# A decoder layer on one core: softplus by ScalarE's own table, and the scan's pieces moved to other stages

## The chip, the core and the metric

The kernel runs on one core of a Trainium2 chip. The metric is the device time of one execution in microseconds (us), the median of several runs. Engines are named as in the profile: PE is TensorE's matmul (PEld its weight load), DVE is VectorE, ACT is ScalarE, POOL is GpSimd, SP issues DMAs.

## The reference

One decoder layer over four batches `b` of 512 rows by 512 columns, all in float32:

```
x = x + attention(layernorm(x))                      # 16 query heads, 2 key/value heads, causal, rotary
x = x + mamba(ctx, gate=layernorm(x))                # selective scan, 512 channels, 16 states
x = x + ffn(layernorm(x))                            # gate/up/down 1408 wide, 8 experts' adapters, top 2
```

The part that the change touches is the selective scan. With `dt = softplus(dt_low @ dt_proj + bias)` and `u` the convolved input, both 512 channels by 512 positions:

```
dt = jax.nn.softplus(dt + dt_proj_b[None, :, None])
state = state * exp(d[..., None] * A) + (d * u)[..., None] * b[:, None, :]
y = einsum('bdn,bn->bd', state, c)                   # 16 states n
y = (y + D * u) * silu(z)
```

## The kernel before

Every engine has its own program, written out by hand, and semaphores tie them. The time runs through these stages, for batch b (of attention and scan) and t (of the feed-forward part):

1. Batch 0 alone: input projection and convolution of the scan, softplus, and eleven places `down0` to `down10` in which PE projects queries, keys and values and DVE rotates them (`rotate`).
2. `attention(b)`: 32 steps, each a pair of heads by one block of 128 query rows. In a step PE makes scores, DVE takes the negated maximum (L1117), ACT the exponent (L622), PE transposes, ACT copies, and PE weighs the values. Scores for step s wait for the exponents of step s - 2. A group of 8 steps goes through the four query blocks, two steps each, with 1, 2, 3 and 4 blocks of keys.
3. `second_sum(t)`, the router, the adapters' masks.
4. 33 evaluations, three for each of the 11 feed-forward tiles f: k = 0 (the base product), 1 and 2 (with one and two experts' adapters). PE fills PSUM, ACT applies Silu (L674), DVE multiplies (L1253). PE's order is adapter 1 of tile f, base product of tile f + 1 (16 matmuls), adapter 2 of tile f, adapter-down product of tile f - 1, and so on; adapter k of a tile waits for the multiplication of evaluation k - 1.
5. Eleven down products `down0` to `down10`, PE's projections of the next batch between them, DVE's rotations beside them, then `finish(t)`, which adds the result to `xb` (L1266) and releases the score banks for the next attention.

Stages 4 and 5 and the attention of batch t + 1 also carry the scan of batch t + 1, cut into pieces. Each piece is one instruction over all 4 channel tiles, 128 x 2048: `mul` (L1077, du times row B), `run` (L1082, the scan itself), `out` (L1087, times row C), 16 of each. Before them come 12 `poly` pieces, which finish softplus: ACT computes |x|, exp(-|x|) and relu(x) of four tiles (`softplus_parts`, L546, L549, L551), and DVE evaluates log1p(e) by a polynomial of degree 9 (one L1051, nine L1054), adds relu (L1059) and multiplies by u (L1063). `plan(counts)` deals the pieces in this order to slots: the 33 evaluations, 11 down places and 32 attention steps. `PLAN_FIRST` serves batch 0, which has no evaluations before it; `PLAN_NEXT` serves batches 1 to 3. For each state the plan also names the slot in which ACT loads rows B and C (`load_bc`, DMA `bc_sb<-bc_rows`, which waits for `out` of state n - 2), the one in which ACT makes the four decays exp(A dt) (`make_decay`, L580, waits for `run` of state n - 2), and the one in which POOL issues the DMA that adds the state into `y_sb` (L484). `mul` of state n waits for that DMA of state n - 2 and for its own rows.

In a slot DVE's program does the evaluation, the maximum or the rotation first and then its pieces, strictly in order. ACT's program does Silu, then loads rows, then decays. Silu, Exp and Softplus stand in different activation tables; ACT_TABLE_LOAD switches between them.

The attention's normalization of the next batch (`deviation`, a POOL power L474, `scaled` L1024) is done four times, once in each of evaluations 18, 21, 24 and 27 (k = 2 of tiles 5 to 8), with a piece between deviation and scaling.

Of the kernel before, what the change touches and what calls it, by code (L numbers as in the profile page):

```python
# [7 lines left out]
ALU = mybir.AluOpType  # L8
# [6 lines left out]
NT = L // P  # L15
# [7 lines left out]
NS = 16  # L23
# [22 lines left out]
def log1p_coefficients(degree):  # L46
    import numpy as np
    nodes = 0.5 + 0.5 * np.cos(np.pi * (np.arange(64) + 0.5) / 64)
    fit = np.polynomial.Chebyshev.fit(nodes, np.log1p(nodes) / nodes, degree, domain=[0, 1])
    return [float(c) for c in fit.convert(kind=np.polynomial.Polynomial).coef]  # L50


POLY = log1p_coefficients(9)
NPOLY = len(POLY)

# [18 lines left out]
NORM_SLOTS = [EVAL_AT[FT - 2 - NT + i, 2] for i in range(NT)]  # L74
DT_SLOTS = (2, 3)
POLY_AT = 4 
LAST_TILE = FT - 1 
# [15 lines left out]
def plan(counts):  # L93

    pieces = [("poly", k) for k in range(NPOLY + 2)]
    for n in range(NS):
        pieces += [("mul", n), ("run", n), ("out", n)]
    assert sum(counts) == len(pieces), (sum(counts), len(pieces))
    slots, at, k = [{"dve": [], "bc": [], "decay": [], "add": []} for _ in range(SLOTS)], {}, 0
    for s, count in enumerate(counts):  # L100
        for piece in pieces[k:k + count]:
            slots[s]["dve"].append(piece)
            at[piece] = s
        k += count
# [11 lines left out]
PIECES = NPOLY + 2 + 3 * NS  # L116
# [75 lines left out]
def decoder_layer(nc, x, ctx_t, wq, wk, wv, wo, w_in, w_x, w_dt, w_lora, w_r, b_down, a_down, w_tiles, w_adapt, w_down,  # L192
                  vectors, constants, out, bc_rows):
    with ExitStack() as stack:
# [63 lines left out]
        u_sb, exp_v, relu_v, conv_sb = state[:, 0, :, :], state[:, 1, :, :], decay[:, 0, :, :], decay[:, 1, :, :]  # L258
        xin_sb = relu_v
# [64 lines left out]
        softplus_chain = sem("softplus_chain")  # L324
        softplus_in = sem("softplus_in")
        y_init = sem("y_init")
        poly_chain = sem("poly_chain")
# [142 lines left out]
        def _(pool):  # L470
# [27 lines left out]
            for t in range(BATCH - 1):  # L498
                inverse_deviation("ffn", t)
                for e in range(EVALS):  # L500
                    inverse_deviation("att", t + 1, [i for i in range(NT) if NORM_SLOTS[i] == e])
# [8 lines left out]
        def _(act):  # L510
# [31 lines left out]
            def softplus_parts(b, tiles):  # L542
                for j in tiles:
                    bank = filled(act, ("dt", j), b)
                    bias = vec[:, V_DTB + j:V_DTB + j + 1]
# [7 lines left out]
                if JT - 1 in tiles:  # L553
                    act.wait_ge(softplus_chain, (b + 1) * 2 * JT)
                    nc.scalar.activation(scrap_a[:], vec[0:1, 0:1], ACT.Copy).then_inc(softplus_in, 1)
# [136 lines left out]
            softplus_parts(0, range(JT))  # L692
# [7 lines left out]
            for t in range(BATCH - 1):  # L700
# [8 lines left out]
                for e in range(EVALS):  # L709
                    if e > 0:  # L710
                        evaluate(t, e)
                    scan_inputs(t + 1, PLAN_NEXT[e])
                    softplus_parts(t + 1, [j for _, j in dt_uses(e)])
# [294 lines left out]
        def _(dve):  # L1008
# [36 lines left out]
            def scan_piece(b, piece):  # L1045
                kind, n = piece
                if kind == "poly":

                    if n == 0:
                        dve.wait_ge(softplus_in, b + 1)  # L1050
                        ts(du_sb[:], exp_v, POLY[-1], None, ALU.mult).then_inc(poly_chain, 1)  # L1051
                    elif n < NPOLY:
                        dve.wait_ge(poly_chain, b * (NPOLY + 2) + n)
                        stt(du_sb[:].rearrange("p j l -> p (j l)"), du_sb[:].rearrange("p j l -> p (j l)"),  # L1054
                            POLY[NPOLY - 1 - n], exp_v.rearrange("p j l -> p (j l)"), ALU.add, ALU.mult)\
                            .then_inc(poly_chain, 1)
                    elif n == NPOLY:
                        dve.wait_ge(poly_chain, b * (NPOLY + 2) + n)
                        tt(dt_sb[:], du_sb[:], relu_v, ALU.add).then_inc(poly_chain, 1)  # L1059
                    else:  # L1060
                        dve.wait_ge(poly_chain, b * (NPOLY + 2) + n)
                        dve.wait_ge(u_ready, b * JT + JT)
                        tt(du_sb[:], dt_sb[:], u_sb, ALU.mult).then_inc(poly_chain, 1)  # L1063

                        nc.vector.memset(decay[:, :, :, 0:1], 0.0).then_inc(dt_ready, 1)
                    return
                base = b * 3 * NS + 3 * n
                flat = state[:, n % 2, :, :].rearrange("p j l -> p (j l)")
                if kind == "mul":
                    if n == 0:  # L1070
                        dve.wait_ge(poly_chain, (b + 1) * (NPOLY + 2))
# [212 lines left out]
            for t in range(BATCH - 1):  # L1284
# [126 lines left out]
```

## Time and profile before

| | |
|---|---|
| Median of 3 runs | 1597.76 us (1597.14 to 1597.82) |
| The profiled execution's own time | 1596.27 us |
| Its span in the profile | 1594.5 us |
| PE busy | 1382.6 us, 87% |
| DVE busy | 1108.9 us, 70% |
| ACT busy | 689.2 us, 43% |
| POOL busy | 112.0 us, 7% |
| Mean granted TensorE clock | 0.888 of full speed |

Busy shares are means over stages with different limits: in the attention of batch 0 DVE is hardly ever idle, while in the feed-forward part of the last batch, which has no scan beside it, it is idle most of the time. The rows below are therefore read stage by stage.

### The profile page before, as it was taken

How to read it: one execution, taken by the hardware profiler on the slowest of the kernel's cores; microseconds unless marked ns; L12 is line 12 of the kernel's file. 1: busy time of each engine (PE TensorE's matmuls, PEld its weight loads, DVE VectorE, ACT ScalarE, POOL GpSimd, SP SyncE). 2: the span in 40 equal slices, each digit the busy share in tenths (PEclk: the TensorE clock that was granted, in tenths of full speed). 3: DMA queues.
4: the chain of work that ended last, by engine and by line, in shares of the span. 5: the costliest groups of instructions: out<-in, count | busy, mean ns of one | idle time of the engine just before them, and what ended most of it. 6: DMA issues, size and time to landing. Idle time of an engine off the chain costs nothing.

```text
span 1594.5 us, 16051 instructions
## 1 busy us (share of the span) xinstructions
PE 1382.6 (87%) x5768; PEld 675.0 (42%) x5768; DVE 1108.9 (70%) x1247; ACT 689.2 (43%) x1501; POOL 112.0 (7%) x116
## 2 busy tenths in 40 slices
PE   6756667999988799899989699899989698799999
PEld 2334334444443355434444255444434255454443
DVE  4899996557989775737999866637998967621120
ACT  6155653344543484343552376361562277321110
POOL 0000001000200000000210000100210000100000
PEclk8955558999999699999999778999999869789999
DMA  4166662114667631113766722002566751101112
GB/s 191 40 152 157 141 142 50 42 50 112 172 145 172 171 68 27 40 35 81 180 147 159 196 67 54 27 32 80 141 150 152 169 139 28 27 19 61 50 35 84
DMA packets 53277, 158.80 MB, mean 100 GB/s; under 512 B 5072, under 2 KB 10704, under 8 KB 44752
## 3 DMA queue, kind: packets, MB, share of 16 engines
q0 software_dynamic: 9216, 67.11, 20.4%
q1 hardware_dynamic: 25664, 54.23, 10.1%
q10 hardware_dynamic: 18320, 36.45, 8.6%
q8 instruction: 47, 0.77, 0.2%
q14 instruction: 30, 0.25, 0.0%
HBM read 86.20 MB, written 4.46 MB: 57 GB/s over the span
## 4 chain that ended last, share of the span: by engine, by line
issue 30%; PE 29%; DVE 26%; DMA 7%; ACT 5%; POOL 2%; ACTq 0%; DVEq 0%; POOLq 0%
DVE state L1082 10%; DMA y_sb<-state 7%; PE ps_a L890 5%; PE ps_a L970 4%; DVE state L1077 4%; PE ps_w L869 3%; DVE state L1087 3%; PE ps_a L816 3%; PE ps_a L902 2%; PE ps_b L830 2%; ACT r L622 2%; POOL rstd L474 2%; DVE neg_max L1117 2%; PE ps_b L910 2%; PE ps_w L778 2%
## 5 line engine op out<-in xcount | busy, mean ns | idle before, releaser
L890 PE MATMUL ps_a<-xt,w_sb 128*128 128x512 f32 x704 | 316.1, 603 | 0.0
L1082 DVE TENSOR_TENSOR_SCAN state<-decay,state 128x2048 f32<-128x2048 f32 x64 | 282.8, 4419 | 7.5 <-ACT decay L580 3.4
L1253 DVE TENSOR_TENSOR r<-r,ps_a 128x512 f32<-128x512 f32 x132 | 88.6, 683 | 206.4 <-ACT r L674 206.4
L816 PE MATMUL ps_a<-r 32*128 32x512 f32 (+3 forms) x512 | 140.6, 634 | 84.0 <-ACT r L622 57.5
L890 PEld LDWEIGHTS ps_a<-xt,w_sb 128*128 128x128 f32 x704 | 135.6, 194 | 171.1 <-issue 171.1
L674 ACT ACTIVATE r<-ps_a 128x512 f32<-128x512 f32 x132 | 78.4, 597 | 297.8 <-PE ps_a L902 158.7
L580 ACT ACTIVATE decay<-dt_sb,decay_rate 128x511 f32<-128x511 f32 x256 | 163.0, 712 | 63.2 <-DVE state L1087 31.2
L622 ACT ACTIVATE r<-ps_a,neg_max 128x128 f32<-128x128 f32 (+3 forms) x256 | 133.8, 534 | 118.7 <-DVE neg_max L1117 118.3
L902 PE MATMUL ps_a<-r,wb_sb 128*128 128x512 f32 x352 | 166.7, 596 | 11.1 <-DVE r L1253 8.9
L970 PE MATMUL ps_a<-wd_sb,r 128*128 128x512 f32 x352 | 161.8, 611 | 0.8 <-DMA wd_sb<-in_w_down 0.8
L1077 DVE TENSOR_TENSOR state<-du_sb,bc_sb 128x2048 f32<-128x2048 f32 x64 | 146.3, 2287 | 5.2 <-DMA y_sb<-state 5.0
L1087 DVE TENSOR_TENSOR state<-state,bc_sb 128x2048 f32<-128x2048 f32 x64 | 146.0, 2281 | 0.7
L830 PE MATMUL ps_b<-cst,r 128*128 128x128 f32 x640 | 120.4, 331 | 25.6 <-ACT xt L634 17.2
L1117 DVE TENSOR_REDUCE neg_max<-ps_a 128x2 f32<-128x256 f32 (+3 forms) x128 | 104.0, 814 | 19.9 <-PE ps_a L819 19.0
L484 POOL DMA_DIRECT2D y_sb<-state x64 | 56.1, 877 | 738.1 <-DVE state L1087 653.4
L902 PEld LDWEIGHTS ps_a<-r,wb_sb 128*128 128x128 f32 x352 | 64.9, 190 | 101.9 <-issue 95.1
L970 PEld LDWEIGHTS ps_a<-wd_sb,r 128*128 128x128 f32 x352 | 69.1, 198 | 88.7 <-issue 84.0
L830 PEld LDWEIGHTS ps_b<-cst,r 128*128 128x128 f32 x640 | 89.1, 172 | 34.5 <-issue 28.7
L816 PEld LDWEIGHTS ps_a<-r 32*128 32x128 f32 x512 | 50.2, 239 | 120.7 <-ACT r L622 79.7
L474 POOL TENSOR_TENSOR rstd<-var_eps,cst 128x1 f32<-128x1 f32 x48 | 56.0, 1167 | 543.7 <-DVE var_eps L1020 534.3
L910 PE MATMUL ps_b<-r,ad_sb 128*128 128x512 f32 x176 | 85.8, 611 | 1.9 <-DVE r L1253 1.7
L1054 DVE SCALAR_TENSOR_TENSOR du_sb<-du_sb,state 128x2048 f32<-128x2048 f32 x36 | 82.4, 2288 | 0.6
(123 smaller groups left out, 1448.4 us busy)
## 6 DMA issues: line engine op xcount, KB each, us to landing
y_sb<-state POOLq DMA_DIRECT2D x64, 1024.0 KB, 9.7
bc_sb<-bc_rows ACTq DMA_DIRECT2D x64, 512.0 KB, 5.1
w_sb<-in_w_tiles SPq DMA_DIRECT2D x44, 512.0 KB, 4.0
wd_sb<-in_w_down SPq DMA_DIRECT2D x44, 256.0 KB, 3.6
wb_sb<-in_w_adapt SPq DMA_DIRECT2D x44, 128.0 KB, 2.1
xa<-in_x SPq DMA_DIRECT2D x4, 1024.0 KB, 5.2
out_x<-xb SPq DMA_DIRECT2D x16, 256.0 KB, 7.0
xn_att<-in_ctx_t SPq DMA_DIRECT2D x4, 512.0 KB, 6.1
```

The costliest lines, as they stand in the source:

```text
L580: nc.scalar.activation(decay[:, n % 2, j, 1:L], dt_sb[:, j, 1:L], ACT.Exp, scale=decay_rate[:, j, n:n + 1]).then_inc(decay_ready, 1)
L622: nc.scalar.activation(probs[:, (2 * s + k) % 4, 0:(i + 1) * P], score_place(s, k), ACT.Exp, bias=neg_max[:, s % 2, k:k + 1], accum_out=ro ...
L816: nc.tensor.matmul(score_place(s, k), q_t[rows, m, i * P:(i + 1) * P], k_t[rows, 0:width], start=True, stop=False, tile_position=(rows.sta ...
L830: mm = nc.tensor.transpose(ps_b[:, k, kt * P:(kt + 1) * P], probs[:, (2 * s + k) % 4, kt * P:(kt + 1) * P], ident)
L890: mm = nc.tensor.matmul(ps_a[:, 2 * (f % 2) + half, :], w_sb[:, slot, at + k * P:at + (k + 1) * P], xt[:, k, :], start=(k == 0), stop=Fals ...
L902: mm = nc.tensor.matmul(ps_a[:, 2 * (f % 2) + half, :], wb_sb[:, f % 2, at:at + P], low[:, 2 * half + k - 1, :], start=False, stop=(k == 2 ...
L910: mm = nc.tensor.matmul(ps_b[:, k - 1, :], ad_sb[:, f, :], hk[:, (2 * f + k - 1) % 4, :], start=(f == 0), stop=(f == FT - 1), skip_group_c ...
L970: mm = nc.tensor.matmul(ps_a[:, i, :], hb[:, f, i * P:(i + 1) * P], wd_sb[:, f % 2, :], start=(f == 0), stop=False, skip_group_check=True)
L1077: tt(state[:, n % 2, :, :], du_sb[:], row, ALU.mult).then_inc(scan_chain, 1)
L1082: nc.vector.tensor_tensor_scan(flat, decay[:, n % 2, :, :].rearrange("p j l -> p (j l)"), flat, 0.0, ALU.mult, ALU.add).then_inc(scan_chai ...
L1087: tt(state[:, n % 2, :, :], state[:, n % 2, :, :], row, ALU.mult).then_inc(scan_chain, 1)
L1117: nc.vector.tensor_reduce(neg_max[:, s % 2, :], both, AX.X, ALU.max, negate=True)\
```

## The change

Softplus becomes one ACT instruction per tile, straight from PSUM into `dt_sb`, and the 12 poly pieces become one piece `du`. The 49 pieces that are left are dealt anew. The normalization moves to evaluations 1 and 3, two tiles in each.

```diff
-NORM_SLOTS = [EVAL_AT[FT - 2 - NT + i, 2] for i in range(NT)]
+NORM_AT = {EVAL_AT[0, 1]: (0, 1), EVAL_AT[0, 2]: (2, 3)}
...
-    pieces = [("poly", k) for k in range(NPOLY + 2)]
+    pieces = [("du", 0)]
...
-        slots[between(at["poly", NPOLY - 4] if n < 2 else at["out", n - 2], at["mul", n])]["bc"].append(n)
-        slots[between(at["poly", NPOLY + 1] if n < 2 else at["run", n - 2], at["run", n])]["decay"].append(n)
+        slots[at["du", 0] if n < 2 else between(at["out", n - 2], at["mul", n])]["bc"].append(n)
+        slots[between(at["du", 0] if n < 2 else at["run", n - 2], at["run", n])]["decay"].append(n)
...
-IN_EVALS = [(0, 2, 1)[k] if e >= POLY_AT and f <= LAST_TILE else 0 for e, (f, k) in enumerate(EVAL)]
-IN_DOWN = 22 
+IN_EVALS = [0 if f == 0 else ((0, 2, 0) if f == 1 else (0, 2, 1))[k] for f, k in EVAL]
+IN_DOWN = 20
...
-EARLY_FIRST = [5, 5]
-IN_DOWN_FIRST = 13 
-PLAN_FIRST = plan([0] * DOWN + EARLY_FIRST + spread_over(IN_DOWN_FIRST - sum(EARLY_FIRST), FT - 2) +
-                  spread_over(PIECES - IN_DOWN_FIRST, STEPS - LAST_STEPS) + [0] * LAST_STEPS)
+PLAN_FIRST = plan([0] * DOWN + [1] * FT + spread_over(PIECES - FT, STEPS - LAST_STEPS) + [0] * LAST_STEPS)
...
-                    nc.scalar.activation(exp_v[:, j, :], ps_w[:, bank, :], ACT.Abs, bias=bias)\
-                        .then_inc(softplus_chain, 1)
-                    act.wait_ge(softplus_chain, (b * JT + j) * 2 + 1)
-                    nc.scalar.activation(exp_v[:, j, :], exp_v[:, j, :], ACT.Exp, scale=-1.0)\
-                        .then_inc(softplus_chain, 1)
-                    nc.scalar.activation(relu_v[:, j, :], ps_w[:, bank, :], ACT.Relu, bias=bias)\
-                        .then_inc(work_free[bank], 1)
...
+                    nc.scalar.activation(dt_sb[:, j, :], ps_w[:, bank, :], ACT.Softplus,
+                                         bias=vec[:, V_DTB + j:V_DTB + j + 1]).then_inc(work_free[bank], 1)
...
+                if kind == "du":
+
+                    for j in (JT - 2, JT - 1):
+                        bank, count = use(("dt", j), b)
+                        dve.wait_ge(work_free[bank], count + 1)
+                    dve.wait_ge(u_ready, b * JT + JT)
+                    tt(du_sb[:], dt_sb[:], u_sb, ALU.mult).then_inc(du_ready, 1)
...
-                    if e in NORM_SLOTS:
+                    for i in NORM_AT.get(e, ()):
                         dve.wait_ge(loaded["x"], 16 * t + 32)
-                        deviation("att", t + 1, xa, NORM_SLOTS.index(e))
+                        deviation("att", t + 1, xa, i)
+                    for i in NORM_AT.get(e, ()):
+                        scaled("att", t + 1, xa, xn_att, i)
```

What `plan` then gives, with m, r and o for mul, run and out and the state's number:

| | before | after |
|---|---|---|
| batch 0, down0 to down10 | 12 poly (10 of them in down0 and down1), m0 | du, m0, r0, o0, m1, r1, o1, m2, r2, o2, m3, one in each |
| batch 0, attention | r0 to o15, 47 pieces | r3 to o15, 38 pieces |
| batches 1 to 3, evaluations | 12 poly in tiles 1 to 4, then m, r at k = 1 and o at k = 2 of tiles 5 to 10, states 0 to 5 | du, m0 at evaluation 4; r, o at k = 1 and m at k = 2 of tiles 2 to 10: r0 to m9 |
| batches 1 to 3, down | m6 to m13, 22 pieces | r9 to o15, 20 pieces |
| batches 1 to 3, attention | r13, o13, m14, r14, o14, m15, r15, o15 in steps 3, 7, 11, 15, 19, 23, 27, 30 | none |

## Rows read from the trace of the kernel before

**Rows 1.** Busy time by stretch: start:end, length, then PE, PEld, DVE, ACT, POOL, clock, DMA.

```profile
80.10:247.10 167.00, 109.55 (x716) 61.46 (x716) 164.59 (x123) 92.83 (x258) 13.32 (x15) 0.57 0.64 147
375.00:387.30 12.30, 12.30 (x30) 5.39 (x29) 10.80 (x9) 9.25 (x13) 0.00 (x0) 1.00 0.21 61
400.00:412.80 12.80, 12.26 (x29) 5.24 (x28) 12.14 (x13) 6.91 (x9) 3.36 (x2) 1.00 0.70 182
1456.80:1540.90 84.10, 84.10 (x197) 37.24 (x196) 14.39 (x22) 12.54 (x21) 0.00 (x0) 1.00 0.17 54
450.70:537.20 86.50, 69.56 (x166) 30.66 (x164) 79.05 (x46) 25.52 (x39) 6.96 (x8) 0.93 0.69 164
537.20:559.60 22.40, 21.42 (x117) 11.20 (x118) 13.83 (x20) 15.62 (x50) 0.00 (x0) 0.52 0.53 166
559.60:614.20 54.60, 48.00 (x564) 29.34 (x562) 39.69 (x64) 41.87 (x149) 1.74 (x2) 0.96 0.23 50
```

**Rows 2.** Groups of DVE instructions: busy us, mean ns, idle before.

```profile
L1082 DVE TENSOR_TENSOR_SCAN state<-decay,state 128x2048 f32<-128x2048 f32 x64 | 282.8, 4419 | 7.5 <-ACT decay L580 3.4
L1077 DVE TENSOR_TENSOR state<-du_sb,bc_sb 128x2048 f32<-128x2048 f32 x64 | 146.3, 2287 | 5.2 <-DMA y_sb<-state 5.0
...
L1054 DVE SCALAR_TENSOR_TENSOR du_sb<-du_sb,state 128x2048 f32<-128x2048 f32 x36 | 82.4, 2288 | 0.6
```

**Rows 3.** Groups of ACT instructions.

```profile
L674 ACT ACT_TABLE_LOAD x28 | 35.9, 1283 | 0.5
...
L546 ACT ACTIVATE state<-ps_w,vec 128x512 f32<-128x512 f32 x16 | 10.9, 680 | 1.1 <-PE ps_w L752 1.1
...
L549 ACT ACT_TABLE_LOAD x7 | 9.0, 1283 | 0.1
```

**Rows 4.** Timeline of batch 0's softplus, ACT, then DVE: start, duration, [idle before].

```profile
27.16 0.67 ACT L546 ACTIVATE state<-ps_w,vec 128x512 f32<-128x512 f32 x1
...
36.37 1.23 DVE L1051 TENSOR_SCALAR du_sb<-state 128x2048 f32<-128x2048 f32 x1 [9.96 <-ACT scrap_a L555]
```

**Rows 5.** DMA issues of the page: count, KB each, us to landing.

```profile
y_sb<-state POOLq DMA_DIRECT2D x64, 1024.0 KB, 9.7
bc_sb<-bc_rows ACTq DMA_DIRECT2D x64, 512.0 KB, 5.1
```

**Rows 6.** Timeline of evaluation tile 7, DVE and PE.

```profile
407.23 4.42 DVE L1082 TENSOR_TENSOR_SCAN state<-decay,state 128x2048 f32<-128x2048 f32 x1
...
411.57 1.26 DVE L1253 TENSOR_TENSOR r<-r,ps_a 128x512 f32<-128x512 f32 x2
...
412.38 1.96 PE L902 MATMUL ps_a<-r,wb_sb 128*128 128x512 f32 x4 [0.54 <-DVE r L1253]
```

**Rows 7.** Timeline of the down stage of t = 0, DVE and PE.

```profile
469.79 0.69 DVE L1099 TENSOR_TENSOR r<-ps_w,cst 128x512 f32<-128x512 f32 x1 [5.16 <-PE ps_w L785]
...
523.24 2.29 DVE L1077 TENSOR_TENSOR state<-du_sb,bc_sb 128x2048 f32<-128x2048 f32 x1 [0.66 <-DMA y_sb<-state]
...
514.55 1.12 PE L799 MATMUL ps_b<-cst,r 128*128 128x128 f32 x4 [7.03 <-ACT r L608]
...
536.06 0.80 PE L816 MATMUL ps_a<-r 32*128 32x128 f32 x4 [9.10 <-DVE xb L1266]
```

**Rows 8.** Timeline of batch 1's attention, DVE: maxima of steps 14, 16, 18, 20, 22, 24.

```profile
572.19 1.22 DVE L1117 TENSOR_REDUCE neg_max<-ps_a 128x2 f32<-128x1024 f32 x1
...
579.55 0.41 DVE L1117 TENSOR_REDUCE neg_max<-ps_a 128x2 f32<-128x256 f32 x1
...
582.89 0.68 DVE L1117 TENSOR_REDUCE neg_max<-ps_a 128x2 f32<-128x512 f32 x1
...
587.13 0.95 DVE L1117 TENSOR_REDUCE neg_max<-ps_a 128x2 f32<-128x768 f32 x1
...
591.43 1.22 DVE L1117 TENSOR_REDUCE neg_max<-ps_a 128x2 f32<-128x1024 f32 x1
...
596.65 0.42 DVE L1117 TENSOR_REDUCE neg_max<-ps_a 128x2 f32<-128x256 f32 x1
```

More of the change, by code:

```diff
@@ L43 @@
 VD = KV_HEADS * HD
[L46 to L54, printed above, removed]
 EVAL = [(0, 0)]
@@ L72 @@
 SLOTS = ATT + STEPS
-NORM_SLOTS = [EVAL_AT[FT - 2 - NT + i, 2] for i in range(NT)]
+NORM_AT = {EVAL_AT[0, 1]: (0, 1), EVAL_AT[0, 2]: (2, 3)}
 DT_SLOTS = (2, 3)
-POLY_AT = 4
-LAST_TILE = FT - 1
 PV_AT = 5
@@ L113, in spread_over @@
     return [(k + 1) * total // places - k * total // places for k in range(places)]
-PIECES = NPOLY + 2 + 3 * NS
-IN_EVALS = [(0, 2, 1)[k] if e >= POLY_AT and f <= LAST_TILE else 0 for e, (f, k) in enumerate(EVAL)]
-IN_DOWN = 22
+PIECES = 1 + 3 * NS
+IN_EVALS = [0 if f == 0 else ((0, 2, 0) if f == 1 else (0, 2, 1))[k] for f, k in EVAL]
+IN_DOWN = 20
 FREE_DOWN = 1
 LAST_STEPS = 1
-EARLY_FIRST = [5, 5]
-IN_DOWN_FIRST = 13
-PLAN_FIRST = plan([0] * DOWN + EARLY_FIRST + spread_over(IN_DOWN_FIRST - sum(EARLY_FIRST), FT - 2) +
-                  spread_over(PIECES - IN_DOWN_FIRST, STEPS - LAST_STEPS) + [0] * LAST_STEPS)
+PLAN_FIRST = plan([0] * DOWN + [1] * FT + spread_over(PIECES - FT, STEPS - LAST_STEPS) + [0] * LAST_STEPS)
 PLAN_NEXT = plan(IN_EVALS + spread_over(IN_DOWN, FT - FREE_DOWN) + [0] * FREE_DOWN +
@@ L256, in decoder_layer @@
         xdt_sb = sb("xdt_sb", [P, L])
-        u_sb, exp_v, relu_v, conv_sb = state[:, 0, :, :], state[:, 1, :, :], decay[:, 0, :, :], decay[:, 1, :, :]
-        xin_sb = relu_v
+        u_sb, xin_sb, conv_sb = state[:, 0, :, :], decay[:, 0, :, :], decay[:, 1, :, :]
         scrap = sb("scrap", [1, 1])
@@ L323, in decoder_layer @@
         bc_stored = sem("bc_stored")
-        softplus_chain = sem("softplus_chain")
-        softplus_in = sem("softplus_in")
         y_init = sem("y_init")
-        poly_chain = sem("poly_chain")
+        du_ready = sem("du_ready")
         dt_ready = sem("dt_ready")
@@ L500, in _ @@
                 for e in range(EVALS):
-                    inverse_deviation("att", t + 1, [i for i in range(NT) if NORM_SLOTS[i] == e])
+                    inverse_deviation("att", t + 1, NORM_AT.get(e, ()))
                     add_states(t + 1, PLAN_NEXT[e])
@@ L540, in split_first, with softplus @@
                                          scale=vec[:, V_D + j:V_D + j + 1]).then_inc(y_init, 1)
-            def softplus_parts(b, tiles):
+            def softplus(b, tiles):
                 for j in tiles:
                     bank = filled(act, ("dt", j), b)
-                    bias = vec[:, V_DTB + j:V_DTB + j + 1]
-                    nc.scalar.activation(exp_v[:, j, :], ps_w[:, bank, :], ACT.Abs, bias=bias)\
-                        .then_inc(softplus_chain, 1)
-                    act.wait_ge(softplus_chain, (b * JT + j) * 2 + 1)
-                    nc.scalar.activation(exp_v[:, j, :], exp_v[:, j, :], ACT.Exp, scale=-1.0)\
-                        .then_inc(softplus_chain, 1)
-                    nc.scalar.activation(relu_v[:, j, :], ps_w[:, bank, :], ACT.Relu, bias=bias)\
-                        .then_inc(work_free[bank], 1)
-                if JT - 1 in tiles:
-                    act.wait_ge(softplus_chain, (b + 1) * 2 * JT)
-                    nc.scalar.activation(scrap_a[:], vec[0:1, 0:1], ACT.Copy).then_inc(softplus_in, 1)
+                    nc.scalar.activation(dt_sb[:, j, :], ps_w[:, bank, :], ACT.Softplus,
+                                         bias=vec[:, V_DTB + j:V_DTB + j + 1]).then_inc(work_free[bank], 1)
             def scan_inputs(b, slot):
@@ L691, in _ @@
             split_first(0)
-            softplus_parts(0, range(JT))
+            softplus(0, range(JT))
             for f in range(FT):
@@ L712, in _ @@
                     scan_inputs(t + 1, PLAN_NEXT[e])
-                    softplus_parts(t + 1, [j for _, j in dt_uses(e)])
+                    softplus(t + 1, [j for _, j in dt_uses(e)])
                 for f in range(FT):
@@ L1046, in scan_piece @@
                 kind, n = piece
[L1047 to L1065, printed above, removed]
+                if kind == "du":
[4 more added lines that the diff above has]
+                    tt(du_sb[:], dt_sb[:], u_sb, ALU.mult).then_inc(du_ready, 1)
+                    nc.vector.memset(decay[:, :, :, 0:1], 0.0).then_inc(dt_ready, 1)
                     return
@@ L1070, in scan_piece @@
                     if n == 0:
-                        dve.wait_ge(poly_chain, (b + 1) * (NPOLY + 2))
+                        dve.wait_ge(du_ready, b + 1)
                         dve.wait_ge(y_init, b * JT + JT)
@@ L1292, in _ @@
                     evaluate(t, e)
-                    if e in NORM_SLOTS:
+                    for i in NORM_AT.get(e, ()):
                         dve.wait_ge(loaded["x"], 16 * t + 32)
-                        deviation("att", t + 1, xa, NORM_SLOTS.index(e))
+                        deviation("att", t + 1, xa, i)
+                    for i in NORM_AT.get(e, ()):
+                        scaled("att", t + 1, xa, xn_att, i)
                     for piece in PLAN_NEXT[e]["dve"]:
                         scan_piece(t + 1, piece)
-                    if e in NORM_SLOTS:
-                        scaled("att", t + 1, xa, xn_att, NORM_SLOTS.index(e))
                 weigh_down(t)
```

## The prediction

> **What bounds the kernel now.** I read the page first, for its slices: the clock granted to TensorE dips in each attention, and no engine is the bound throughout. So I cut the span into stages [rows 1]. Four things are to be seen there. In the attention of batch 0 DVE is busy for 164.6 of 167.0 us while PE is at 109.6: DVE is the bound. In the evaluations of the last batch, which carry no scan, seven tiles take 84.1 us with PE busy all the time, 12.0 us each: PE is the bound. An evaluation tile with a scan state and a normalization takes 12.8 us with DVE at 12.1; one with a scan state alone takes 12.3 with DVE at 10.8 and PE never idle. The down stage takes 86.5 us with DVE at 79.1 and PE at 69.6: DVE again. The attention of batch 1, with 8 pieces, takes 22.4 us for its first 8 steps, PE at 21.4 and the clock at 0.52, hence nearly all of it at 1.2 GHz, and 54.6 for the steps up to the last maximum, clock 0.96, PE at 48.0, DVE at 39.7, ACT at 41.9: there no engine is full, and the loop from engine to engine is the bound.
>
> **The change, part by part.** A mul, an out and a poly piece cost 2.29 us, a run 4.42 [rows 2], so a state costs 9.0. The 12 poly pieces of a batch are at most 12 x 2.29 = 27.5 us of DVE, du is one product of the same size, 2.3 (I take out, du and mul as equal). So 25 us a batch, about 100 us in all, leave DVE. What that is worth is read stage by stage.
>
> *Batch 0, up to attention.* Softplus: 12 instructions of some 0.68 us [rows 3] become 4. The trace has no Softplus. From below it costs the 0.68 of a 128 x 512 instruction with the same bias, from above the three that it replaces, 2.0. I take 0.68, since shape, source and bias are those of L546. ACT's part runs from 27.2 to 36.4, where DVE gets its first piece after 10.0 us idle [rows 4]; with 8 x 0.65 us less, and PE half waiting on it, it ends near 33. But m0 now waits for rows B and C, which ACT issues only after the four copies that follow softplus, at about 37.5, and which land 5.1 us later [rows 5]: DVE idles from 35.5 to some 42.7. The stage's DVE work is du + 4 mul + 3 run + 3 out = 31.7 us, and rotations and the value copy, 11. From 33: 33 + 31.7 + 11 + 7.2 = 82.9, against 80.1, where attention begins now. So +2.8 us (-3 to +6: the order of bc, decay and copies on ACT can cost or give as much again).
>
> *Batch 0, attention.* Nine pieces fewer, three states: -27.0. DVE idles 2.4 us now; one piece to a step is less even, and with the clock low a step takes 22.4 / 8 = 2.8 us without DVE being the bound, against 3.5 of DVE for a mul with its maximum. I add 2. So -25 (-29 to -16). Together with the line above: **-22 us**.
>
> *Evaluations, three times.* Pieces per tile and slot are the same 6.7 us at k = 1 and 2.3 at k = 2, now in tiles 2 to 10. In the tiles with a normalization the run ends at 411.6, two multiplications follow back to back, and PE has waited 0.54 us for them [rows 6]; DVE's 12.1 + waits fill 12.8. Without the normalization DVE has 10.8, and PE's 12.0 should set the pace. Four tiles give 4 x 0.8 = -3.2. The normalization's new places, evaluations 1 and 3, lie where PE does the dt products and the projection; I count some 4.3 us of DVE and POOL in each, inside idle time of 5 to 6 us. Where that cover is gone, it costs 4.3 once. ACT's Softplus loads stay as many as the Exp loads they replace (7), and Silu's return is the same, but each of ten decay slots now costs one load of Exp and one of Silu instead of six: 25 more loads, 25 x 1.283 = 32 us of ACT [rows 3]. In a tile they hide: ACT does 7 of 12 us now in such a tile, loads included [rows 1]. One place is exposed: at evaluations 4 to 6 du, m0 behind the rows' 5.1 us, and decay 0 with two loads come in sequence; I count PE waiting 1.5 + 0.7 us, against about as much that dt's banks and the first poly pieces cost now. Zero. So **-3.2 each** (-6 to +5; the upper end is nine tiles at 12.8 instead of four, and 1 for the start).
>
> The Trainium skill says otherwise on the price of a table switch: "ScalarE: Activation LUTs", What ACT_TABLE_LOAD costs, gives some 2.66 us for one with its drain. The trace shows 1.283 [rows 3], and Silu starts right after it. By the page's figure evaluations 4 to 6 would lose another 3 us a batch and the sum would be -67, an estimate from that page.
>
> *Down stage, three times.* 22 pieces (8 mul, 7 run, 7 out, 65.2 us) become 20 (6, 7, 7, 60.7): -4.5. DVE waits 5.2 us for the first rotation's matmul, because only four pieces stand before it [rows 7]; now they are r9, o9, m10, r10, 13.4 us instead of 11.3: -2.1. Against that, DVE without rotations runs a state in 9.1 us, and mul n waits for the addition of state n - 2, which lands 9.7 us after its issue [rows 5], and I add 0.2 from out to issue: 0.8 us for m14 and m15 each, and one wait of 1 for the second rotation, 0.7 there now: +1.1. So **-5.5 each** (-8 to -1). PE's end of the work isn't the limit: it waits 9.1 us for `finish`, and 7.0 before that for ACT, which stands behind a wait for an out [rows 7]. That place is kept (the loading of B and C for state 15 waits for o13) and comes some 3 us sooner.
>
> *Attention, three times.* Eight pieces, 24.7 us of DVE, go. The price of one is read in pairs of steps [rows 8]. Without a piece: one block 3.3 us (579.55 to 582.89), three blocks 4.3 (587.13 to 591.43). I put two blocks at 3.85 and four at 4.75 in line with these. Four blocks with a run take 7.4, so a run costs 2.6; four blocks with a mul take 5.2, two with an out 4.2, so one of these costs 0.4. A group of 8 steps without pieces is then 16.2; from step 8 to the last maximum I get 16.2 + 16.2 + 13.8 = 46.2 (the last one without its final step, 2.4), against 54.6: -8.4. The first 8 steps are PE-bound at the low clock: they keep PE's 21.4, -1.0. So **-9.4 each** (-4, if the loop was limited elsewhere, to -15, if the clock rises sooner).
>
> Sum: -22 - 3 x (3.2 + 5.5 + 9.4) = -76.3. The profiled execution took 1596.3 us, 1.8 more than its span; that gives 1520.0. The median is 1.5 above it: 1521.5. In my count most errors are waits left out, so I say **1523 us**.
>
> **The rivals.**
> 1. *Attention stays bound by PE and clock.* PE waits 9.1 us before the first scores and the clock is low for the 22 us after [rows 1, 7]. If that lasts, or its dips come again without the pieces, attention gives 3 us a batch: -22 - 3 x 11.7 = -57, 1541 us. For it: PE at 21.4 of 22.4 and 48.0 of 54.6. Against: PE's 7 idle us there come behind runs. 0.17.
> 2. *The clock comes back sooner.* With denser steps and a shorter wait before the first scores, part of the 22 slow us runs at 2.4 GHz; PE's part would be worth up to some 6 us a batch: -94, 1504 us. 0.13.
> 3. *The scan sets the pace of nine tiles*, not four: each at 12.8, or with ACT's two loads late for Silu k = 0. That is +4 to +7 instead of -3.2: -76 + 3 x 8 = -52, 1546 us. For it: the one tile with a scan alone takes 12.3, not 12.0 [rows 1]. 0.08.
> 4. *Slower than before.* ACT becomes the bound of the 27 scan tiles. The rest of the change gives 67 us, so a tile would have to take 12.0 + 70 / 27 + 0.4 = 15.0 us, that is, two table loads of more than 3.5 us each beyond ACT's slack; at 15.5 it is 1611 us. Every load in the trace takes 1.283 [rows 3]. 0.02.
> The forecast itself 0.60.
>
> **How the numbers follow.** A measurement of this kernel can tell about 0.2%, 3.2 us, from no change. The bounds of the terms together would reach from 1482 to 1580, but they don't come all at once. The range reaches down to rival 2 and up to rivals 1 and 3: 1502 to 1548; the forecast's own is 1511 to 1535. Only rival 4 isn't a gain, and between it and the others lies a cent for no change: faster 0.97, same 0.01, slower 0.02.
>
> **What would show it.** No L1054 group; 16 Softplus instructions near 0.68 us; table loads up by 25; batch 0's attention starting near 83 and some 142 us long, DVE still above 95%; tiles at 12.0 us with PE full; down stage near 81 us; attention from first to last maximum near 68 us, with groups of 8 steps near 16. The prediction is wrong if the tiles stay at 12.8 or more, if mul waits for `y_sb` in every down place, or if PE fills attention at the low clock.

## The result, and the profile after

The changed kernel takes 1521.77 us (median of 4 runs, 1517.45 to 1524.04) against 1597.79 before: ratio 0.951, 95% interval 0.947 to 0.955. I had said 1523. The profiled execution took 1524.03 us, its span is 1522.2 against 1594.5, so the two traces differ by 72.3 us; the profiled execution is one of the two slower ones of the four, and the medians differ by 76.0.

Busy time by stretch, as in [rows 1]: attention of batch 0; an evaluation tile; the down stage of t = 0 from the weighing to the first maximum; the first eight steps of batch 1's attention; the rest of it.

```profile
91.20:231.00 139.80, 106.00 (x709) 60.42 (x710) 138.48 (x113) 82.73 (x241) 10.52 (x12) 0.58 0.66 141
...
393.30:405.30 12.00, 12.00 (x29) 5.32 (x28) 10.79 (x7) 6.91 (x9) 0.89 (x1) 1.00 0.74 188
431.40:511.50 80.10, 70.88 (x166) 31.29 (x165) 74.52 (x43) 17.06 (x27) 6.07 (x7) 0.93 0.67 159
511.50:533.00 21.50, 21.25 (x114) 11.23 (x114) 7.67 (x17) 13.38 (x46) 0.00 (x0) 0.50 0.59 166
533.00:580.30 47.30, 46.25 (x567) 29.23 (x566) 23.25 (x58) 40.81 (x146) 0.00 (x0) 0.99 0.01 2
```

DVE is still the bound in the first (138.5 of 139.8 us) and nearly so in down (74.5 of 80.1); in the tile PE is busy all the time; in the attention of batch 1 it now nearly is, in the first steps at 1.2 GHz.

Groups of ACT instructions, which answer to [rows 3]:

```profile
L642 ACT ACT_TABLE_LOAD x40 | 51.3, 1283 | 0.7
L548 ACT ACT_TABLE_LOAD x34 | 43.6, 1283 | 0.6
L522 ACT ACTIVATE dt_sb<-ps_w,vec 128x512 f32<-128x512 f32 x16 | 10.2, 684 | 2.4 <-PE ps_w L720 2.3
L522 ACT ACT_TABLE_LOAD x7 | 9.0, 1283 | 0.1
```

Softplus costs 684 ns, the lower of my bounds, and the loads are 40 + 34 + 7 where they were 28 + 21 + 7: 25 more, as counted.

Where the 72.3 us come from, by the starts of the same instructions in both traces (sums over the batches):

| stretch | before | after | difference | forecast |
|---|---|---|---|---|
| start to batch 0's first maximum | 80.1 | 91.2 | +11.1 | +2.8 |
| batch 0, first to last maximum | 167.0 | 139.9 | -27.1 | -25 |
| three times, second sum to weighing | 536.1 | 527.9 | -8.2 | -9.6 |
| three times, weighing to first maximum | 258.4 | 240.2 | -18.2 | -16.5 |
| three times, first to last maximum | 233.7 | 206.1 | -27.6 | -28.2 |
| four times, last maximum to second sum | 109.8 | 104.5 | -5.3 | 0 |
| last batch, from its second sum | 209.4 | 212.6 | +3.1 | 0 |

The last two rows hold code that the change doesn't touch, but the first of them follows from the change. Of the 109.8 us before, the clock is at 1.2 GHz for 18.9, because it falls around the last maximum; after, for 0.6. Batch 0's stretch goes from 26.1 to 24.2 us, and it is 24.2 in every kernel with this plan for batch 0. Those of batches 1 to 3 go from 28.1, 28.1 and 27.5 to 27.1, 27.1 and 26.1, and att8, which puts the eight pieces back, has 28.1, 28.1 and 27.5 again. The last row differs between executions of the same code (209.2 to 212.6 in the traces of this document).

Batch 0 before attention, timeline of DVE: start, duration, [idle before and its end].

```profile
36.42 2.29 DVE L1021 TENSOR_TENSOR du_sb<-dt_sb,state 128x2048 f32<-128x2048 f32 x1 [9.02 <-issue]
...
43.92 2.29 DVE L1035 TENSOR_TENSOR state<-du_sb,bc_sb 128x2048 f32<-128x2048 f32 x1 [5.18 <-DMA bc_sb<-bc_rows]
...
58.05 0.69 DVE L1057 TENSOR_TENSOR r<-ps_w,cst 128x512 f32<-128x512 f32 x1 [4.28 <-PE ps_w L753]
...
88.98 2.29 DVE L1035 TENSOR_TENSOR state<-du_sb,bc_sb 128x2048 f32<-128x2048 f32 x1 [1.55 <-DMA y_sb<-state]
```

Here 12.0 us go by in waits for other engines and DMAs after du, where I had 7.2: the rows' 5.2 as said, then 4.3 for rotation 1's matmul, 1.6 for the addition into `y_sb`, and three of 0.2 to 0.4. Why that matmul is late shows on ACT: eight decays in one slot stand ahead of the second projection's move. PE waits 3.37 us for this move and then makes the third projection at 1.2 GHz, in 6.57 us; in first_fix, where it didn't wait, the same took 3.70.

```profile
44.95 5.00 ACT L548 ACTIVATE decay<-dt_sb,decay_rate 128x511 f32<-128x511 f32 x8
49.86 0.67 ACT L570 ACTIVATE r<-ps_w,q_bias 128x512 f32<-128x512 f32 x1
...
50.58 6.57 PE L746 MATMUL ps_w<-xt,wq_sb 128*128 128x512 f32 x8 [3.37 <-ACT r L570]
```

In the evaluations one place got worse, tile 1 (evaluations 3 to 6: 15.0 us, 11.6 before). ACT and PE there:

```profile
316.35 1.28 ACT L548 ACT_TABLE_LOAD   x1
317.64 2.56 ACT L548 ACTIVATE decay<-dt_sb,decay_rate 128x511 f32<-128x511 f32 x4
320.21 1.28 ACT L642 ACT_TABLE_LOAD   x1
321.51 1.08 ACT L642 ACTIVATE r<-ps_a 128x512 f32<-128x512 f32 x2
...
322.97 7.11 PE L858 MATMUL ps_a<-xt,w_sb 128*128 128x512 f32 x16 [2.13 <-DVE r L1211]
```

Two Silus come back to back, of evaluations 6 and 7: the first had waited behind decay 0 and its two loads, and PE waited 2.13 us for its product.

### The profile page after: what moved, and what is told of

The parts are those of the page before. It is cut to its first block, busy times and chain, and to the rows that moved or that the text cites. A ratio compares the mean times of both kernels' runs of the same rounds, so it can differ in the third digit from the quotient of the medians.

```text
span 1522.2 us, 15997 instructions
## 1 busy us (share of the span) xinstructions
PE 1368.4 (90%) x5768; PEld 673.0 (44%) x5768; DVE 1021.4 (67%) x1203; ACT 701.7 (46%) x1490; POOL 89.6 (6%) x116
## 4 chain that ended last, share of the span: by engine, by line
PE 66%; DVE 21%; ACT 6%; issue 4%; DMA 3%; ACTq 0%; DVEq 0%; POOL 0%
PE ps_a L858 21%; PE ps_a L870 9%; DVE state L1040 8%; PE ps_a L938 5%; PE ps_b L878 5%; PE ps_a L784 5%; PE ps_w L837 4%; PE ps_b L798 3%; DVE state L1035 3%; PE ps_w L746 3%; DMA y_sb<-state 3%; DVE state L1045 3%; PE ps_w L904 2%; ACT r L590 2%; DVE neg_max L1075 2%
## 5 line engine op out<-in xcount | busy, mean ns | idle before, releaser
L858 PE MATMUL ps_a<-xt,w_sb 128*128 128x512 f32 x704 | 320.0, 609 | 6.4 <-DVE r L1211 6.4
L784 PE MATMUL ps_a<-r 32*128 32x512 f32 (+3 forms) x512 | 137.0, 620 | 51.6 <-ACT r L590 34.2
L798 PE MATMUL ps_b<-cst,r 128*128 128x128 f32 x640 | 117.1, 325 | 15.2 <-ACT r L602 7.8
L1088 DVE TENSOR_TENSOR r<-ps_w,r 128x128 f32<-128x128 f32 x64 | 18.4, 287 | 78.1 <-ACT r L609 78.1
L602 ACT ACTIVATE xt<-ps_b 128x256 f32<-128x256 f32 (+1 forms) x128 | 57.9, 504 | 24.0 <-PE ps_b L798 23.4
```

The source lines that it names most:

```text
L784: nc.tensor.matmul(score_place(s, k), q_t[rows, m, i * P:(i + 1) * P], k_t[rows, 0:width], start=True, stop=False, tile_position=(rows.sta ...
L798: mm = nc.tensor.transpose(ps_b[:, k, kt * P:(kt + 1) * P], probs[:, (2 * s + k) % 4, kt * P:(kt + 1) * P], ident)
L858: mm = nc.tensor.matmul(ps_a[:, 2 * (f % 2) + half, :], w_sb[:, slot, at + k * P:at + (k + 1) * P], xt[:, k, :], start=(k == 0), stop=Fals ...
```

## The experiments

Theory: VectorE time is worth only what the stage's own bound leaves, so the gain is the room made by the poly pieces times the price of a piece in the stage that is emptied. Rivals: VectorE's total counts; or the clock does. Each ratio is to the kernel before, on the same chip, with its 95% interval. Executions of the kernel before differ by up to 13 us on one chip, so below 5 us the trace's stages decide, and not the medians. The helper `move_decay(plan, n, slot)`, which some edits call, puts the decays of state n into another slot; `...` marks lines of an edit that are left out.

**softplus_alone.** Table softplus with the plan and the normalization of before:

```diff
-NORM_AT = {EVAL_AT[0, 1]: (0, 1), EVAL_AT[0, 2]: (2, 3)}
+NORM_AT = {EVAL_AT[FT - 2 - NT + i, 2]: (i,) for i in range(NT)}
...
-IN_EVALS = [0 if f == 0 else ((0, 2, 0) if f == 1 else (0, 2, 1))[k] for f, k in EVAL]
-IN_DOWN = 20
+IN_EVALS = [int((f, k) == (4, 2)) if f < 5 else (0, 2, 1)[k] for f, k in EVAL]
+IN_DOWN = 22
-PLAN_FIRST = plan([0] * DOWN + [1] * FT + spread_over(PIECES - FT, STEPS - LAST_STEPS) + [0] * LAST_STEPS)
+PLAN_FIRST = plan([0] * DOWN + [int(f in (7, 10)) for f in range(FT)] + spread_over(PIECES - 2, STEPS - LAST_STEPS) +
+                  [0] * LAST_STEPS)
...
```

> The changed kernel with the plan and the normalization of before: table softplus, du in the place of the last poly piece, every scan piece in its old slot (22 in down, 8 in attention, 47 in batch 0's attention). Theory (the gain comes from the room that the poly pieces leave and that scan pieces then fill): taking the poly pieces away in evaluation tiles 1 to 4, where PE sets the pace at 12.0 us, gives nothing; only batch 0 gains, where ten poly pieces held up the rotations, 10 to 14 us. So 1584 to 1589 us; attention of batches 1 to 3 stays at 77 to 78.5 us from first to last maximum, down at 83 to 84. Rival (VectorE's total time is what counts, 100 us less of it gives 75): near 1525.

Measured: 1581.58 us, 0.991 (0.987 to 0.994). Batch 0's attention begins at 68.9 us, 11.2 sooner, and takes 168.4; down (weighing to `finish`) stays at 83.0 to 83.5. So the some 96 us of instructions that leave VectorE give about 16 (10 to 20 by the interval), and the rival falls. Not expected: evaluations 0 to 3 took 21.7 to 22.8 us and not 25.5, 3 us a batch, since ACT gives PE the banks of dt sooner: before, PE waited 0.72 and 0.69 us for them between its dt products, and now it doesn't. The trace after has that too (22.8). Not expected either: the attention of batch 2 took 84.6 us, while the two others took 78.1 and 77.7. Its clock was at 1.2 GHz for 17.1 us of steps 16 to 23, where it was for 3.4 in the two others; why, no run shows.

**att8.** Eight pieces back in attention, in their old steps.

```diff
-IN_DOWN = 20
+IN_DOWN = 12
```

> The changed kernel with IN_DOWN = 12 in place of 20: the last 8 pieces stand in attention again, in the same steps as before. Theory: attention of batches 1 to 3 goes from 68.7 back to about 78 us (+9.2 each), but the down stage, now bound by VectorE at 77.5 us with 20 pieces, falls until PE's own work of about 69.5 us bounds it (-7.5 each); net +1 to +3 a batch, 1525 to 1531 us. Rival (pieces cost in attention what they cost in down, or attention was bound by the clock and not by pieces): attention stays under 72 us and the whole comes out at 1505 or less.

Measured: 1514.71 us, 0.947 (0.943 to 0.952), where I had expected it above the changed kernel's; the two intervals overlap. Attention is back at 76.7 to 77.2 us, +8.3 each, and the stretch behind its last maximum is 1.1 longer again, as before the change. By groups of eight steps the pieces cost nothing in the first, 2.7 in the second (m14 and r14; 3.0 by my prices), 1.1 in the third (o14 and m15; 0.8) and 4.9 in the last (r15 and o15; 3.0), where the clock falls for some 4 us and doesn't without them. But the down stage falls from 80.1 to 70.1 us up to the first maximum, -10.0, more than I allowed. Busy time of its down stage and the attention's first steps:

```profile
431.40:501.70 70.30, 67.69 (x164) 29.71 (x163) 50.64 (x36) 14.69 (x23) 3.47 (x4) 1.00 0.57 132
501.70:522.90 21.20, 15.62 (x114) 8.82 (x115) 14.11 (x21) 15.18 (x50) 0.03 (x1) 0.78 0.47 156
```

Down is bound by PE now. The net of these stages is 8.3 + 1.1 - 10.0, about -0.6 us a batch: a tie, in which a piece costs about as much in down as in attention. The rest of the 7 us between the medians isn't theirs: 3.4 us of the difference between the traces lie in the last batch and 2.0 up to the weighing, where both kernels have the same code. That a better split exists is shown by down16 and not by this run.

**norm_late.** The normalization back in evaluations 18 to 27, with a piece between deviation and scaling.

```diff
-NORM_AT = {EVAL_AT[0, 1]: (0, 1), EVAL_AT[0, 2]: (2, 3)}
+NORM_AT = {EVAL_AT[FT - 2 - NT + i, 2]: (i,) for i in range(NT)}
...
```

> The changed kernel with the normalization back in evaluations 18, 21, 24, 27, one tile each. Theory: four evaluation tiles go from 12.0 back to 12.8 us, +3.2 a batch, and the start of the evaluations gets nothing back, since the normalization lay in idle time there: +9 to +10 us in all, 1531. Rival (the 12.8 us came from the pieces' order, mul and run at k = 1, and not from the normalization): tiles stay at 12.0 to 12.2 and the time within 2 us of the changed kernel's.

Measured: 1524.50 us, 0.954 (0.951 to 0.958). Four tiles take 12.7 us again, DVE at 12.1 in the one from 391.0 to 403.7, PE no longer full:

```profile
391.00:403.70 12.70, 12.22 (x29) 5.24 (x28) 12.14 (x12) 6.91 (x9) 3.43 (x2) 1.00 0.70 178
```

So the normalization with a piece inside it, not the order mul and run at k = 1, made the 12.8. From second sum to weighing the three batches lose only 1.3 us each on average (175.9, 177.3, 178.4 against 175.9), not 3.2: the tiles lose 0.7 each, 0.6 comes back between evaluations 30 and 32, and in the first of the three batches 2.4 before evaluation 3. So the whole is 2.7 us above the changed kernel, where I had said 9 to 10; the place of the normalization is worth some 4 us in all by the stages.

**first_fix.** In batch 0 rows B and C are loaded ahead of softplus, decays 0 and 1 apart.

```diff
+move_decay(PLAN_FIRST, 0, DOWN)
+move_decay(PLAN_FIRST, 1, DOWN + 2)
...
+            load_bc(0, PLAN_FIRST[DOWN])
             softplus(0, range(JT))
...
```

> The changed kernel with two edits for batch 0 alone: rows B and C of states 0 and 1 are loaded ahead of softplus, and the decays of state 0 are made in down0, those of state 1 in down2 (both stood in down1, ahead of the second projection's move). Theory: the 11 us that batch 0 lost up to attention are 5.2 for the rows, 4.3 for rotation 1 behind the eight decays, the rest clock and start. Without the two, attention begins 7 to 9 us sooner, near 83, and the time falls as much, to 1513 to 1516. Rival (the delay is PE's low clock in that stretch, and the waits only its face): attention begins at 88 or later, the time falls by under 3 us.

Measured: 1516.91 us, 0.949 (0.945 to 0.953), attention from 85.8. That looks like most of it, but isn't: in this execution du began at 33.8, in the changed kernel's at 36.4. From du to the first maximum it is 52.0 us against 54.8, so the edits give 2.8. The rows' wait is gone (du 33.8, mul 36.2); DVE then stood 2.6 us for ACT's move and 2.9 for PE's rotation product instead. The third projection then ran at 2.4 GHz, and rotation 1 had no wait:

```profile
36.16 2.29 DVE L1046 TENSOR_TENSOR state<-du_sb,bc_sb 128x2048 f32<-128x2048 f32 x1
41.09 0.69 DVE L1065 TENSOR_TENSOR r<-r,cst 128x512 f32<-128x512 f32 x1 [2.63 <-ACT r L579]
44.66 0.69 DVE L1068 TENSOR_TENSOR r<-ps_w,cst 128x512 f32<-128x512 f32 x1 [2.88 <-PE ps_w L764]
...
44.54 3.70 PE L757 MATMUL ps_w<-xt,wq_sb 128*128 128x512 f32 x8
```

The 7 to 9 us that I expected were too many: a wait taken away was followed by the next one in the queue. By the number this is my rival's outcome (under 3 us), but the rival's cause was only a part: of the 4.3 us wait for rotation 1, 2.9 are the low clock in the third projection, and that came behind ACT's move.

**decay0_later.** Decays of state 0 at evaluation 6.

```diff
+move_decay(PLAN_NEXT, 0, EVAL_AT[1, 2])
```

> The changed kernel with one edit: for batches 1 to 3 the decays of state 0 are made at evaluation 6 and not at evaluation 5. Theory: PE's wait of 2.13 us before tile 3's base product ends, because Silu of evaluation 6 no longer stands behind two table loads and four exponents; evaluations 3 to 6 take 12 to 13 us in place of 15.0, and 2.1 to 3 us a batch come off, 6 to 9 in all: 1513 to 1516 us. Rival (the start of the evaluations is held by du and the first mul on VectorE): evaluations 3 to 6 stay at 14 or more, under 2 us in all.

Measured: 1514.02 us, 0.944 (0.940 to 0.948). Evaluations 3 to 6 take 11.0 us, but 6 to 9 take 13.6 (10.3 before the edit). Evaluation 0 to weighing, both from the start of the multiplication: 145.3, 145.7, 145.2 against 147.1 to 147.3, -1.8 a batch. The cause is right, but 3.3 of the 4.0 us come back in the next tile; that 1.8 are left is due to tile 3 (11.4 for 12.0) and 0.5 less behind evaluation 32.

**more_loads.** A third table load in each of the 30 decay slots beside evaluations.

```diff
+                for n in slot["decay"]:
+                    at = b * NS + n
+                    nc.scalar.activation(scrap_a[:, at:at + 1], vec[0:1, 0:1], ACT.Softplus)
                 make_decay(b, slot)
```

> The changed kernel with a Softplus of one element ahead of the decays in each of the 30 decay slots beside evaluations, so that each has three table loads instead of two (1.28 + 0.19 us more of ScalarE a slot, 44 us in all). Theory (table loads hide in the tiles, since ScalarE has slack before Silu of k = 0 and PE has 3.4 us of other work after its base product): the tiles stay at 12.0 us; only the exposed place, decay 0 at evaluation 5, passes the 1.5 us on, so +4 to +5 us in all, 1526. Rival (ScalarE is at the edge in a tile, as the one that makes this change slower would need): tiles go to 12.8 or more and the time by 20 us or more.

Measured: 1531.63 us, 0.955 (0.951 to 0.959), some 6 us above what I expected. Tiles 3 to 9 stay at 12.0 with ACT at 8.4:

```profile
396.00:408.00 12.00, 12.00 (x29) 5.32 (x28) 10.81 (x7) 8.40 (x11) 0.89 (x1) 1.00 0.75 191
```

Tile 1 goes from 15.0 to 16.5, as expected, and the stretch from evaluation 32 to weighing from 3.5 to between 4.4 and 5.3, which I had left out; one tile 2 took 12.0 and not 10.3. From second sum to weighing the three batches take 10.2 us more in all. Rival 4 of the prediction is far off: even a third load costs at the two ends of the evaluations alone, and nothing in tiles 3 to 9.

**down16.** 16 pieces in down, four in attention steps 1, 3, 5, 7.

```diff
-IN_DOWN = 20
+IN_DOWN = 16
+ATT_AT = (1, 3, 5, 7)
...
-                 spread_over(PIECES - sum(IN_EVALS) - IN_DOWN, STEPS - LAST_STEPS) + [0] * LAST_STEPS)
+                 [ATT_AT.count(s) for s in range(STEPS)])
```

> The changed kernel with 16 pieces beside the down products and the last four (o14, m15, r15, o15) in attention steps 1, 3, 5 and 7. Theory (the down stage is bound by PE at 66.9 us with 12 pieces and by VectorE above some 16; the first eight steps take 21 us with and without pieces): down 67 to 69 us, attention from first to last maximum 68.5 to 71, so 7 to 9 us a batch below the changed kernel and 5 to 7 below the one with 8 pieces in attention: 1495 to 1500 us. Rival (a piece costs in the first steps what it costs in the later ones, or more where it lies on every second step): attention 73 us or more, 1507 or more.

Measured: 1513.55 us, 0.944 (0.940 to 0.949). Attention takes 68.6 to 68.8, its first eight steps 21.7: the four pieces there cost 0.2 us, as good as free, as expected. Down (weighing to `finish`) takes 73.1 to 73.7, 4 us less than in the changed kernel, not 67 to 69. PE stands before its last product:

```profile
492.47 6.69 PE L939 MATMUL ps_a<-wd_sb,r 128*128 128x512 f32 x8 [5.62 <-DMA wd_sb<-in_w_down]
```

That load was issued at 482.97 and landed at 492.42; the 1 MB addition into `y_sb` was issued at 481.94 and landed at 492.25. PE then made the product at 1.2 GHz, in 6.69 us, where it took 3.60 for those before. The bound was neither of my two. The other traces agree: in the 14 of them 341 loads of `wd_sb` were issued while an addition was in flight, and all landed 0.2 to 3.1 us after this addition. In the changed kernel one issued at 480.6 landed at 489.6, the addition of 479.4 at 489.4, and PE didn't stand for it; in att8 one of 487.5 landed at 493.8, the addition of 483.5 at 493.4. In the last batch, which has no additions, the eleven loads take 2.6 to 3.4 us. No run moves the load alone.

**down16_fixed.** down16, first_fix and decay0_later in one kernel.

> The kernel with 16 pieces in down and four in the first attention steps, together with the two edits for batch 0 and the later decays of state 0. Theory: the three gains lie in different stages and add up: 7.5 x 3 + 5 + 7 = 34 us below the changed kernel, 1485 to 1492 us. Rival (they share a limit, or the clock takes some back): 1497 or more.

Measured: 1498.67 us, 0.935 (0.931 to 0.939). Down 72.5, attention 68.4, du to first maximum 51.9, evaluation 0 to weighing 144.5. The number lies where I had put the rival (1497 or more), but the stages show no shared limit: the three gains are all there, and a little more. What is missing to my number is down16's and first_fix's shortfall.

**best.** Decays of state 1 at evaluation 9 as well.

```diff
+move_decay(PLAN_NEXT, 1, EVAL_AT[2, 2])
```

> The fixed kernel with 16 pieces in down, and the decays of state 1 made at evaluation 9 instead of 7. Theory (in decay0_later the stall only moved to tile 2, 13.6 us, because ScalarE had four table loads between the Silus of evaluations 6 and 8): tiles 1 to 3 at 11.0, 12.0 to 12.5 and 12.0, another 1 to 1.5 us a batch: 1494 to 1497 us. Rival (tile 2 is held by something else): 13.6 stays and so does 1498.7.

Measured: 1499.89 us, 0.938 (0.936 to 0.939): the same as the run before. Tile 2 stays at 13.6. Its trace shows that ACT is free there now, but Silu of evaluation 7 still waits for decay 0, so run and out of state 0 take DVE from 321.3 on, and evaluation 8's product waits for them until 328.0; PE loses 0.80.

**warm**, **best_warm**, **warm10.** Matmuls with unused results on PE ahead of the first scores of batches 1 to 3: six in the changed kernel, three in the kernel just told, ten in the changed kernel.

```diff
                 pe.wait_ge(v_ready, b + 1)
+                if not first_batch(b):
+                    for k in range(6):
+                        nc.tensor.matmul(ps_b[:, 1, :], wx_sb[:, k % JT, :], xt[:, k % KT, :], start=True, stop=True)
```

> The changed kernel with six more matmuls of 128 x 512 (results unused) on PE between the last output product of a batch and the first scores of the next, about 5.2 of the 5.5 us in which PE waits there. Theory (the 21.5 us of the first eight attention steps, against 16.2 to 16.5 later, come from the low clock, and the clock is low because PE waited): the clock stays at 2.4 GHz into the attention and the first eight steps take 16 to 18 us, 10 to 15 us less in all, 1507 to 1512. Rival (the steps themselves let the clock fall: with 8 pieces in attention PE entered it without a wait, at the high clock, and the first eight steps still took 21.2): the first steps at most 1 to 2 us shorter, the whole within 4 us of the changed kernel's.

> The kernel of the run before with three more matmuls of 128 x 512 (results unused) before the first scores, where PE hardly waits any more. If the clock of the first steps can be held by that, 3 us a batch or more come off (under 1488); if the steps themselves let it fall, the three cost their own 2.6 us a batch less what wait there is: 1497 to 1503.

> As the run with six more matmuls before the first scores, but with ten, 8.6 us: with six PE still waited 3.0 us and the clock had fallen 1.8 us before the first maximum, so that run told nothing. Theory (the low clock comes from PE's wait): PE enters attention at 2.4 GHz, keeps it, and the first eight steps take 16 to 18 us. Rival (the steps let it fall): PE enters at 2.4 GHz, the clock falls within them all the same, the first eight steps take 19 to 21.5 us. In both the matmuls themselves cost 0 to 1 us a batch.

With six: 1517.62 us, 0.948 (0.946 to 0.951); PE still waited 3.0 us, the clock fell at 505.9, ahead of the first maximum at 507.7, and the first eight steps took 21.5. That tells nothing on the cause. With three in the other kernel: 1507.93 us, 0.943 (0.941 to 0.945), 8 us worse, which is the three times 2.5 us by which the first maximum comes later behind `finish`. With ten: 1515.99 us, 0.949 (0.945 to 0.952), and the profile of one execution shows the clock held and lost. Batch 1's first eight steps and its rest, then the first steps of batches 2 and 3:

```profile
507.90:522.70 14.80, 13.14 (x124) 7.67 (x124) 7.80 (x19) 12.92 (x47) 0.00 (x0) 1.00 0.86 242
522.70:568.40 45.70, 44.59 (x556) 27.60 (x555) 23.09 (x58) 40.34 (x146) 0.00 (x0) 1.00 0.01 2
854.50:874.90 20.40, 19.30 (x114) 10.21 (x114) 7.86 (x17) 12.99 (x46) 0.00 (x0) 0.58 0.56 162
1206.00:1226.40 20.40, 19.22 (x113) 10.21 (x114) 7.87 (x17) 12.98 (x46) 0.00 (x0) 0.58 0.52 139
```

All three batches entered at 2.4 GHz. One kept it and took 14.8 us; in the two others the clock fell 3.4 us in, and they took 20.4. So neither side of my pair holds alone. All traces together say it more sharply. In 24 attentions of batches 1 to 3 PE waited 3 to 9 us before the first scores, and in all 24 the clock was at 1.2 GHz by the first maximum. In 18 it didn't wait (att8, the kernels with 16 pieces in down, warm10), and in all 18 the clock was at 2.4 GHz there; but in 17 of them it fell 2 to 12 us later.

## Why the prediction came out right, step by step

**Total.** 1523 forecast, 1521.8 measured; the likeliest case is the one that came. But part of the closeness is luck. In the trace the gain is 72.3 us for my 76.3: batch 0 was off by 6, evaluations by 1.4 and attention by 0.6 against me, down by 1.7 for me, and the stretches that I had put at nothing by 2.2 (-5.3 and +3.1). The median then lies 2.3 us below the execution that was profiled. The four executions themselves differ by 6.6 us.

**Batch 0, up to attention: mis-sized.** The step "33 + 31.7 + 11 + 7.2 = 82.9, against 80.1" came out at 91.2. Two of its terms failed. The waits were 12.0 us in place of 7.2; I had named the order of bc, decay and copies as the danger and had not followed it through, which would have shown the second projection's move (raw 1) behind eight decays. And du began at 36.4 and not 33: the scan's low projection reached ACT 2.8 us later than before, PE at the low clock for 6.8 us from 18.9 on where the trace before has 3.4, and ACT waited 2.3 us on PE's dt products. That is no oddity of this execution: in seven of the eight traces of kernels with this start du begins at 35.8 to 36.4, and only in down16, where the clock didn't fall there, at 31.3, with attention from 86.1. So of the 8.3 us beyond the forecast 4.8 are the missed waits and 3.4 the later du, by the clock.

**Batch 0, attention: right.** -27.1 for 27.0 of pieces; DVE idles 1.3 us, not 4.4, so the less even plan, for which I had added 2, cost nothing. With the step above, -16.0 in place of -22.

**Evaluations: right in sum (-2.7 each for -3.2), wrong in parts.** The tiles gave 12.8 to 12.0 as said, and in norm_late they are 12.7 again. I had set off 1.5 + 0.7 us of PE waiting at the start against what softplus costs there now, to zero: it is -2.7 from softplus in evaluations 0 to 3 (softplus_alone) and +2.3 in evaluations 3 to 9, most of it PE's wait of 2.1 behind decay 0. What I had left out is some +0.9 from evaluation 30 to the weighing, a place where more_loads shows that loads cost. The 5.1 us wait of m0 for its rows didn't come: ACT's queue issued the DMA at 308.9, ahead of Silu 4, which stands before it in the program, while the engine was still computing. Table loads hide in the tiles, as said (more_loads). The Trainium skill ("ScalarE: Activation LUTs", What ACT_TABLE_LOAD costs) adds a drain of 1.38 us to each load; in no run here is there one: the Softplus behind the load of 302.61 begins at 303.91, but for the kernel's first load the engine is never idle for more than 0.02 us ahead of one in the trace after, and all 121 loads of more_loads are of 1.283.

**Down: right (-6.1 each for -5.5).** 4.5 for the two pieces, the rest from the first rotation's wait, which went from 5.2 to 2.3 us. What I didn't see is that eight pieces cost the stage 10.0 us (att8), no less than the 9.4 that they cost in attention and behind it, while four of them are as good as free in attention's first steps (down16).

**Attention: right (-9.2 each for -9.4).** The groups of eight steps took 21.5, 18.0 and 16.5; I had 21.4, 16.2 and 16.2, and the last one 12.7 for 13.8. So the sum is right by terms that offset each other. My prices give 6.8 us for the six pieces behind step 8, and I had taken 8.4; att8 has 8.6, since run and out in the last group cost more than the pairs of steps showed, and bring the low clock with them.

**Behind attention: a term put at nothing.** The stretch from the last maximum to the second sum gave 5.3 us. The clock no longer falls there (18.9 us at 1.2 GHz before, 0.6 after), and for batches 1 to 3 att8 shows that this comes and goes with the pieces in attention.

**Rivals 1 and 2, the clock.** Neither came. warm10 shows how near rival 2 is: 60.5 us for one attention in place of 68.7. That it depends on PE's wait alone, as I had it, isn't so.

What stays open: what lets the clock fall within the first steps of attention in 17 of 18 cases, and hold in one; why the scan's low projection of batch 0 meets the low clock in all traces but down16's; and why down's weight load lands only with the addition into `y_sb`.

## What to carry to other kernels

Price an instruction by the stage that it leaves and the one that it enters: 96 us of VectorE were worth 16 where they stood, and 76 once other work had moved into the room. When pieces move, walk each queue behind the move: the losses here were a projection's move behind eight exponents and a Silu behind two table loads, both on an engine at 46%. After a gain look for the best split again: 16 pieces in one stage and four in steps that PE bounds, with the queue edits of first_fix and decay0_later, give 1498.7 us, 1.5% below the changed kernel.

## What the runs showed of the hardware

- In down16 a 256 KB weight load lands in 3.3 us as a median, but one that was issued 1 us behind a 1 MB accumulating DMA of another queue took 9.4, and both landed within 0.2 us; in the last batch, without such DMAs, these loads take 2.6 to 3.4. All 341 that were issued while such a DMA was in flight, in 14 traces, landed after it.
- ACT's queue issued a DMA while the engine still computed what stands before it in the program: at 308.93, right after PE's product for Silu 4 had ended at 308.83, and 2 us before that Silu began at 310.97.
- Where PE had waited before attention the clock was at 1.2 GHz at the first maximum in 24 cases of 24, and where it hadn't in none of 18.
- The same eight attention steps took 14.8 us at 2.4 GHz throughout, 20.4 where the clock fell 3.4 us in (both in one execution of warm10), and 21.5 at 1.2 GHz throughout.
